# A transformer layer on one core: another order of the pieces of work, and a wait by name for the buffers of probabilities

## What is computed

```python
B, S, D, H, FF, E, K = 2, 512, 256, 16, 1024, 8, 2       # 77 keys in cross-attention
def _attn(q_in, k_in, v_in, ..., causal):
    scores = einsum('bqhd,bkhd->bhqk', Q, Kp) / sqrt(HD)
    if causal: scores = where(tril, scores, -inf)
    a = softmax(scores)
    return einsum('bhqk,bkhd->bqhd', a, V).reshape(...) @ wo + bo
x = _layernorm(x + _attn(x, x, x, sa_..., True), ln1_g, ln1_b)
x = _layernorm(x + _attn(x, encoder_output, encoder_output, ca_..., False), ln2_g, ln2_b)
x = _layernorm(x + _moe(x, ...), ln3_g, ln3_b)           # top 2 of 8 by router softmax, exact gelu
```

## Time and profile before

| | |
|---|---|
| median of 3 runs | 755.05 us (754.03 to 757.26) |
| span of the profiled execution | 755.9 us |
| TensorE busy | 711.2 us, 94% |
| VectorE busy | 499.0 us, 66% |
| ScalarE busy | 369.2 us, 49% |
| GpSimd busy | 287.3 us, 38% |
| chain that ended last | TensorE 75%, issue 8%, VectorE 7%, DMA 5% |

### The profile page before, as it was taken

One profiled execution on the slowest core, in us unless ns is written; L12 is line 12 of the kernel. 1 busy time (PEld: TensorE's weight loads), 2 busy tenths in 40 slices (PEclk: granted clock), 3 DMA queues, 4 the chain that ended last, 5 costly groups with the idle time before them and its releaser, 6 DMA issues.

```text
span 755.9 us, 14560 instructions
## 1 busy us (share of the span) xinstructions
PE 711.2 (94%) x4969; PEld 478.4 (63%) x4969; DVE 499.0 (66%) x1376; ACT 369.2 (49%) x749; POOL 287.3 (38%) x558
## 2 busy tenths in 40 slices
PE   6889999999999999999997889999999999999983
PEld 4444434545464454645563666898999999999941
DVE  5679788678766877756687744365666665666436
ACT  4325475665666676677753436433433332332403
POOL 8305521542653463624654333212332332232114
PEclk9999999999999999999997989999999999999997
DMA  8954431343164021316037762676999999999754
GB/s 273 291 145 128 114 98 46 84 129 128 34 179 127 13 60 48 92 43 179 14 113 237 223 210 95 204 262 226 357 328 343 343 326 341 343 332 333 236 187 163
DMA packets 95154, 140.29 MB, mean 186 GB/s; under 512 B 11855, under 2 KB 81077, under 8 KB 92597
## 3 DMA queue, kind: packets, MB, share of 16 engines
q1 hardware_dynamic: 76357, 107.86, 45.5%
q10 hardware_dynamic: 15072, 22.02, 9.1%
q0 software_dynamic: 3648, 9.45, 3.5%
HBM read 110.65 MB, written 28.65 MB: 184 GB/s over the span
## 4 chain that ended last, share of the span: by engine, by line
PE 75%; issue 8%; DVE 7%; DMA 5%; POOL 2%; ACT 1%; SPq 0%; DVEq 0%; ACTq 0%; POOLq 0%
PE out_acc L984 11%; PE score_pair L961 10%; PE work L932 9%; PE score_pair L855 8%; PE work L849 8%; PE work L906 6%; PE work L855 4%; PE score_pair L849 3%; PE work L1008 3%; DVE neg_part_max L1472 3%; PE work L918 2%; PE work L992 2%; PE work L935 2%; DMA arena<-parts_scratch 1%; PE out_acc L849 1%
## 5 line engine op out<-in xcount | busy, mean ns | idle before, releaser
L1472 DVE TENSOR_REDUCE neg_part_max<-work 128x1 f32<-128x512 f32 (+4 forms) x368 | 213.3, 625 | 70.4 <-PE work L935 35.9
L1244 ACT ACTIVATE arena<-score_pair 128x1024 f32<-128x1024 f32 (+2 forms) x224 | 178.9, 839 | 79.8 <-PE score_pair L961 78.9
L932 PE MATMUL work<-arena 96*128 96x77 bf16 (+4 forms) x640 | 118.5, 278 | 10.3 <-ACT arena L1207 2.7
L961 PE MATMUL score_pair<-arena 99*128 99x512 bf16 (+2 forms) x448 | 104.2, 337 | 4.0 <-DMA arena<-negmax_scratch 3.0
L984 PE MATMUL out_acc<-arena 128*32 128x512 f32 (+4 forms) x896 | 103.7, 517 | 2.6 <-DVE arena L1492 2.6
L1904 POOL DMA_INDIRECT chosen_scratch<-arena,scatter_rows x36 | 35.6, 989 | 176.5 <-DVE arena L1404 176.2
L855 PE MATMUL score_pair<-arena 128*128 128x256 f32 x432 | 97.6, 380 | 0.0
L932 PEld LDWEIGHTS work<-arena 96*128 96x128 bf16 x640 | 49.5, 99 | 74.5 <-issue 31.0
L1960 POOL TENSOR_SCALAR_AFFINE_SELECT arena<-arena 128x256 f32<-128x256 f32 x128 | 51.5, 410 | 117.9 <-ACT arena L1244 116.7
L1177 ACT ACTIVATE arena<-work,expert_b_cols 128x128 f32<-128x128 f32 x180 | 51.1, 369 | 77.3 <-PE work L849 64.0
L849 PE MATMUL work<-arena 128*128 128x128 f32 x720 | 87.7, 279 | 0.3 <-issue 0.3
(11 more groups left out here) (257 smaller groups left out, 955.0 us busy)
## 6 DMA issues: line engine op xcount, KB each, us to landing
arena<-in_L_xattn_e_w SPq DMA_DIRECT2D x54, 1024.0 KB, 7.1
arena<-parts_scratch SPq DMA_DIRECT2D x24, 768.0 KB, 6.1
arena<-in_L_xattn_e_w ACTq DMA_DIRECT2D x18, 1024.0 KB, 6.4
parts_scratch<-arena_more SPq DMA_DIRECT2D x24, 384.0 KB, 2.6
parts_scratch<-arena_more SPq DMA_DIRECT2D x24, 256.0 KB, 3.0
parts_scratch<-arena_more SPq DMA_DIRECT2D x24, 128.0 KB, 2.9
residual<-in_x SPq DMA_DIRECT2D x4, 512.0 KB, 8.1
tokens_scratch<-residual SPq DMA_DIRECT2D x2, 1024.0 KB, 5.4
```

The costliest lines, as they stand in the source:

```text
L932: m = pe.matmul(bank[:, j * it.w:(j + 1) * it.w], qa[st.half(it.g)][0:R_S, h, n0:n0 + P], k, start=True, stop=not it.last)
L961: m = pe.matmul(st2[pair][0:rows, j, 0:w], k, qa[st.half(it.g)][0:R_M, h, skip:QG], start=True, stop=True)
L1244: act_e.activation(pt[buf][0:rows, :, 0:w], st2[pair][0:rows, :, 0:w], ACT.Exp, scale=float(HD) ** -0.5).then_inc(pair_taken[pair], 1)
L1472: dve.tensor_reduce(pm[:, it.at, it.t, it.h0:it.h0 + it.nh], bank[:, 0:it.nh * it.w].rearrange("p (j k) -> p j k", j=it.nh), AX.X, ALU.max ...
```

## The change

The string `ORDER` is another one. It holds the same pieces, kind by kind in the same order, so that the instructions are the same. 392 of the 969 pieces with work on TensorE stand elsewhere in its order, 91 of 429 on ScalarE, 85 of 551 on VectorE, 39 of 239 on GpSimd and 14 of 63 on SyncE. And one line is new in ScalarE's program, at score. Scores may now stand ahead of the weigh that frees their buffer as far as TensorE is concerned; in the new line that is so for 24 of the 112 weighs, which have three later scores ahead of them, where before at most two were.

```diff
@@ -262,18 +262,18 @@
 ORDER = (
-    "x6prbpxvrs2lxvcp2crsrsp2vrm6xm3xm2xm6lvm3pm4rpm3gym2im4xm2qm5qmxqm3f3m2qfwmqmqmwxrm2qsqsfxm3fwm2qm3f2wxmrqm2"
...
+    "sx3sx3prbprxvxvlcpsrpcpm3r2mpmsm3rvgm3fxfm2xm2xm5vm4fp2slfm3rmym3smixmxm3qmsmq2m2fm2qm2fqfm2wfqm2xm2fmwrfxmqmqm2wm"
...
 )
@@ -1238,6 +1238,7 @@
                     e.wait_ge(pair_full[pair], it.n // 2 + 1)
 
+                    e.wait_ge(prob_taken[buf], it.n // 4)
                     if it.n == 2:
                         e.wait_ge(self_apart, 2)
                         e.wait_ge(cross_apart, 2)
```

More of the change, by code:

```diff
@@ L275 @@
-    "udpdA3rpt2NADWsrNA2lU2so2lt2n3NBn4onUBhVYyUnonNZn3qnqnenha3U2YyR2wuZMaMq2dYR2qwAuq2M2AHNAwudqUwuUd2PZtNtotot"
-    "o2eU2YaZa3zNUYR2LRLRUZNKLSLCHUYPKSTUZNU2YUZUEOIA3XDY2Z2W"
+    "sx3sx3prbprxvxvlcpsrpcpm3r2mpmsm3rvgm3fxfm2xm2xm5vm4fp2slfm3rmym3smixmxm3qmsmq2m2fm2qm2fqfm2wfqm2xm2fmwrfxmqmqm2wm"
+    "wfxm2qm3qmqm2qpum2wf2mfrmfq2smwmq2lm4wm2pygm3pmwum2dqfdqm2qfmfmwmqmqm3qm2wmqmqm2wqm2rmqfmwmqsqmf2mwmgmqmqmlwqfqf2"
+    "m2rmqwf2qfsf2umfm2wmqfmqmwmqfm2f2rmqmwymq2sm3fwm2lq2m2wm2qm2fqfmfwmsqm2frqmwf2qmqm2wuqmqwmqpmvpm2qwqm3qwfqmdmqwmqd"
@@ new lines @@
+    "mq2flmwmugmpqm2wym2fqfwmfqmfm2qpmqmqwmdqm2fwmuqmrqmwm2qm2qmrwmq2mdfmwm3q2m2wt2q2moftfmgqmfswfmo2q2mfwmsqtqfw2mfqmq"
+    "uomefqf2mf3qfmwqm2fmwmqm2qwmrfqmyfmq2wmqwq2m2fqfmwadfqm2wpm2qwlqm2umfaqvfm2aq2m2wmqmwqfm3q2fwsm2dq2mjtwumafqgvxfm2"
+    "wxfqx2m2swytoqtopqmpmfqfrfmqwfmqmum2tqwm2qwm2orqf3rlfsfgmfm2fqwqm2qmwmqmqm2wpqmqrmwmqm2q2mwpmwm2oq3nm2qulwmfqndqm2"
+    "w2eafqsamsmdqnfqmwnqfqmfnyhwnqfmnfqnam2fafqswfm3q2mwf2qf2wm2q2m2vlfmywqudmfmqxfrw2m2xf4q2dx2qvmslmfwqmqm2wnqmumpmq"
+    "duwqnqnmqumnqnmwmnqmwmq2mpgnwqdnqywnwdfufdyivfnt2hnrosto2tq2onuqnqwlqnquewqnqwqa3dwqnx2qaqnhdnwqxnqnywnxfwnqfnhnft"
@@ L277 @@
+    "qptoqrq2twsf2yqpqfuwlfwortqofqpqowserusuq2wdqpqd2wanua2n3uqwnqnqdRdqnwtRwtnotqsrqho2atMqwoeqMRlRq2wfMnyMfqanHf3q2w"
+    "aqfPafKSfRwvMaqhnqRwnqn2wquMRdqMRn2tMtHqzoywouvtPKdotoueSqwqFwBq2uawasXxdxlOa2xsBkuxIdpA2rdAptlNADWtNrA2U2o2tNnBn3"
+    "otn2UBVonhnYynUNn3eqn2anqZnUha2UYR2wyauqZM2YR2q2AuMdqwMq2duAwHNAUuwUd2tPZt2o2to2aNaU2YaeZzNUaYR2LRLRUZNKLSLCHUYPKS"
+    "TUZNU2YUZUEOIA3XDY2Z2W"
 )
```

## The result

The changed kernel takes 779.6 us (median of 4 runs, 774.45 to 782.35) against 754.99 of the kernel before on the same chip: a ratio of 1.0311, 95% interval 1.0264 to 1.0358. It is slower by some 24 us, where I had forecast no change.

The account below looks back on a forecast made before the run. TensorE was taken as the bound, busy 711.2 of 755.9 us, with VectorE bounding some stretches. The parts summed to -0.3 us on the median 755.05, giving some 754.7, range 749.0 to 759.8.

Parts of the forecast that it names:

- Part 3: First maxima, 20 to 80 us: moving them early taken as 0; +3.5 if TensorE decides, -2 if VectorE's idle time shrinks.
- Part 1: ScalarE's Exps: the added wait costs 0.07 us at 18 places where TensorE waited, +1.3; ends 0 and 6.5.
- Part 2: TensorE, whole kernel: fewer changes of matmul shape, going to weigh 108 times instead of 111, -0.5 us.
- Rival B: Up to 80 us: early idle makes moved work not fit TensorE's stalls, +3.5, total 759.4 us; chance 0.12.
- The cover that I claimed for SyncE: Early maxima: S0.g1's load, some 3 us later behind a store, stays hidden under 32 maxima; uncovered, +3.
- Part 4: 80 to 318 us: earlier bank requests and less work between S4.g0's keys and maximum, +1 us; ends 0 and +4.7.
- Part 5: 318 to 388 us: shorter small waits against S6's keys arriving late, together -2.1 us; ends -4.8 and -1.
- The reliefs: 318 to 388 us: S5.g1's load -0.9, cross-attention weighs -1.3, router's product -0.5, S6.g0's small waits -0.4 us.
- Part 6: 392 to 411 us, bounded by VectorE: a copy ahead of two routing operations saves 0.3 us; ends -1 and +1.5.
- Part 7: 418 to 480 us: later maxima transfer +0.9, later load +0.3, earlier router turns and prefix step -0.9; sum +0.3.
- rows 3: Earlier profile's list of TensorE's waits; a new wait over 2 us missing from it would prove the forecast wrong.
- the sign of the tenths: 80 to 318 us: the forecast is wrong if TensorE's busy tenths fall under 9.

Follow-up runs that it names:

- e3: Changed kernel with the first eight maxima of S0.g0 put back behind projection S1.q0 and values S1.0: 777.80 us, ratio 1.0273 to the kernel before.
- e11: Order of before plus the added wait, with only the first eight maxima of S0.g0 moved early: 764.92 us beside 756.55 or similar runs, ratio 1.0106.
- e10: Order of before plus the added wait, with only c_rank and c_place moved directly behind c_prefix: 762.51 us beside 756.55, ratio 1.0074.
- e7: Changed kernel with its six longest TensorE stalls filled with unused transposes, order and waits kept: 772.27 us, ratio 1.0194 to the kernel before.
- e2: Changed kernel with the loads of S1.g0 and S7.g0 put back ahead of the stores: 777.56 us, ratio 1.0253 to the kernel before.
- e1: Kernel before, its order unchanged, with only ScalarE's added wait: 757.69 us beside 757.62, ratio 1.0005.
- e4: First 940 pieces in the new order, the rest in the order of before, added wait kept: ratio 1.0131 to the kernel before.
- e8: Changed kernel with the first four maxima of S6.g0 moved 1.8 us of work later: 777.12 us, ratio 1.0241 to the kernel before.
- e9: Changed kernel with all the named moves of maxima, loads, c_rank and c_place taken back: 767.80 us, ratio 1.0137 to the kernel before.
- e5: First 940 pieces in the order of before, the rest in the new order, added wait kept: ratio 1.0146 to the kernel before.
- e12: First 940 pieces in the order of before, the rest as in e9: 767.40 us, ratio 1.0136 to the kernel before.
- e16: Order of before to piece 940, then e9's order up to c_rank, then the order of before again: ratio 1.0115 to the kernel before.
- e14: Order of before up to 385 us, from there the new order, added wait kept: 758.04 us, ratio 1.0022 to the kernel before.
- e15: e11 with 32 unused transposes filling TensorE's idle time ahead of the first maximum: 760.80 us beside 756.02, ratio 1.0049.
- e6: Kernel before, without the added wait, with two TensorE idle times filled by unused transposes: 757.93 us beside 757.16, ratio 1.0008.

## Why the prediction was wrong, point by point

The forecast was 754.7 in a range up to 759.8; the time is 779.6, outside it. In one sentence: the sum put at nothing what the early maxima cost (Part 3), had no term for c_rank and c_place on VectorE and for two loads behind stores on SyncE (S1.g0, S7.g0), and priced no stall with the stretch at the lower clock behind it. The runs show 2.9 (e3) to 8.0 us (e11) for the first, 5.6 (e10) for the second, 9 for the lower clock behind six stalls (e7), which overlaps with the others, and for the two loads together 4 us, not clear of 0 (e2).

- **Part 1, the wait** (+1.3, ends 0 and 6.5): right, and at its low end, 1.0005 in e1. 18 waiting places became 25.
- **Part 2, changes of shape** (-0.5): too small to be seen in any run. Its working has a slip: eight products two at a time are 4 x 0.11 = 0.44, not 0.48, which makes a change 0.13 and the term -0.8.
- **Part 3, the first maxima** (taken 0, end +3.5): the step that failed is the sentence "If VectorE decides, its start and its work are the same: 0". VectorE was at 45.23 of 51.6 before and is at 42.62 now; with the moved projection and values between the maxima, TensorE feeding it more slowly fits that, though no run shows it by itself. Rival B named the place and the mechanism, with a chance of 0.12, but priced it at the wait alone: +3.5, where e11 alone measured +8.0, some 3 to 4 of it the clock. The cover that I claimed for SyncE I checked only for the load of S0.g1. I did not ask the same of the load of S1.g0, which the new line puts behind the store of S1.g1's queries: issued at 78.70 instead of 55.12, and the changed kernel's trace lost 3.3 us near there, of which e4 and e8 have 1.2 and 1.5.
- **Part 4** (+1, ends 0 and +4.7): 3.0 measured between 139 and 302 us, spread; e9, in which this part is as in the new line, has 2.9 there too. With the 3.3 at 90 us, which lies in this part's stretch and which it had no term for, the trace has 6.3, outside the ends.
- **Part 5** (-2.1, ends -4.8 and -1): the keys of S6 were priced at 1.0 and the wait is 1.58, so the step was right in kind and near in size; the stretch at the lower clock that followed, 365 to 372 us, was not in the sum. The reliefs are real but small: e5, e12 and e16, which have the old front, gain 0.9, 1.3 and 1.2 us between 348 and 355 us in their traces, after losing 0.6 to 0.7 between 330 and 348, for my 3.1. The part came out at +3.2, outside its ends.
- **What the sum left out altogether**: 371 to 385 us, +7.4. The load of S7.g0 stands behind the store of S7's keys, and c_rank and c_place stand ahead of the maxima of S7.g0. I compared TensorE's order there and did not go through VectorE's and SyncE's piece by piece. e10 prices the second at +5.6 us. For the first, e2 shows the wait gone but no time of its own. The wait of 1.79 us and the 14 us at half the clock behind it, 389 to 403 us, are up to some 9 us by themselves; how they and c_place share the loss there no run shows.
- **Part 6** (-0.3, ends -1 and +1.5): +2.4 measured, and e14 prices all behind 385 us at 1.7, not clear of 0, when it is reached in time.
- **Part 7** (+0.3): 1.2 between 401 and 422 us and nothing behind it; right in the rest.
- **The clock**: "I am wrong if a wait of over 2 us appears that rows 3 do not have" came true, with 3.53, and so did the sign of the tenths, with the 8 at 78 to 97 us. But I read the lower clock of the earlier trace rows only as something that might be won, and not as a price on each new stall. That is the main term missing: filling six stalls (e7) gave back 9 of 24 us with the order and the waits as they were.

What stays open: nearly half of the loss is not bound to single moves. With all the named moves taken back the kernel is still 1.37% slower than before (0.77 to 1.97), and its trace puts some 6 us of that at 385 to 401 us, where the new order by itself costs 1.7. That the backlog of VectorE and the lower clock act on each other there is how I read it; the later place of c_rank and c_place in e9 is the rival, and no run takes them apart. No version here beats the kernel before.

## What to carry to other kernels

When all work stands in one line, a move has to be followed on every engine's list: the two questions that would have found most of this are which store each load now stands behind on its queue, and which long piece of VectorE now stands ahead of one that empties a bank. Where TensorE is full, a lag stays; it is given back only where TensorE waited anyway (e16: 11.7 us behind at 439 us and 6.4 at 453, where the kernel before waits 2.8 us for a transfer). So to put pieces that need a transfer ahead of work that doesn't is a loss even if the engine behind them looks like the bound. A new stall of TensorE is to be priced above its length: the 3.20 us of e10 cost 5.6, and the 3.8 us that e11 adds to the wait ahead of the first maximum cost 8.0. And where one trace per kernel is compared, run the same order more than once before a difference of 2 us is explained.

## What the runs showed of the hardware

- Idle times of 1.6 to 1.8 us already stood ahead of stretches at 1.2 GHz (364.40 and 388.48 in the changed kernel), and these ran for 7 and 14 us. The earlier trace rows had 1.38 us of idle time with no such stretch behind it, and 1.25 us ahead of 87.37 in the changed kernel had one. The length alone doesn't decide: the idle time at 528 us is 1.32 before, with the clock at 1.00 behind it, and 1.44 in e1, with 0.50.
- Executions of one kernel differ in mean clock and in time: 23 of the kernel before on one chip run from 754.52 us at 0.988 to 762.34 at 0.982, and the four of e9 from 764.35 at 0.985 to 771.87 at 0.974.
- Useless transposes in place of idle time kept the clock at 2.4 GHz (e15: 1.00 for 0.57 from 27 to 35 us) and, by the times, halved the stall's price, though the intervals overlap; filling six in the changed kernel gave 9 us (e7). In the kernel before they changed no time (e6, 1.0008).
- The two operations of c_place took 2.31 us together in the changed kernel and 2.30 in e10, but 1.30 in e16, with the same shapes. GpSimd's tensor_tensor operations of 128x256 ran beside them in the first two (L1999, 0.72 us, and L2001, 1.05) and casts and operations of 128x32 in e16. That the one slows the other is read from these traces; no run was made to test it.
